# Attention + FP4 feed-forward on one core: the row maximum of two score banks taken as two steps of 512 columns and a join, instead of one step of 1024

## The reference, cut to what matters

```python
# attention, 4 batches x 1024 rows x 128; 16 heads of 64
m = jnp.max(s, axis=-1, keepdims=True)          # <- the row maxima of the scores
e = jnp.exp(s - m)
attn = e / (jnp.sum(e, axis=-1, keepdims=True) + EPS)
x = x + (attn @ v) @ Wo.T + bo                   # q, k, v from layernorm(x)
# then a gated feed-forward whose inputs and weights are rounded block by block to FP4
h = jax.nn.silu(fp4_linear(x, w_gate)) * fp4_linear(x, w_up)
x = x + fp4_linear(h, w_down)
```

## Time and profile before

| | |
|---|---|
| median of 3 runs | 1841.92 us (1841.74 to 1843.65) |
| the profiled execution | 1839.61 us, of which the span of the trace is 1837.8 us |
| TensorE busy, weight loads | 90%, 66% of the span |
| VectorE busy | 84% |
| GpSimd busy | 68% |
| ScalarE busy | 59% |
| TensorE clock granted, mean | 0.967 of full speed |
| max steps, `sm` matmuls | 512 and 1024 |

### The profile page before, as it was taken

One profiled execution on the slowest core, in us unless ns is written; L12 is line 12 of the kernel. 1 busy time (PEld: TensorE's weight loads), 2 busy tenths in 40 slices (PEclk: granted clock), 3 DMA queues, 4 the chain that ended last, 5 costly groups with the idle time before them and its releaser, 6 DMA issues.

```text
span 1837.8 us, 41990 instructions
## 1 busy us (share of the span) xinstructions
PE 1649.2 (90%) x13825; PEld 1205.2 (66%) x13825; DVE 1544.5 (84%) x2591; ACT 1078.5 (59%) x2222; POOL 1241.5 (68%) x1369
## 2 busy tenths in 40 slices
PE   4899999999999989999999998989989898999966
PEld 2566677677666666666666666666666666766754
DVE  7888887777888979789797888888888888898877
ACT  3566666666656656566565565655656555666533
POOL 3577777777776766676666766666666666677753
PEclk7999999999999999999999999999999999999987
DMA  5111101111011110011110011100111000111000
GB/s 128 25 24 24 24 17 23 24 25 24 13 26 26 26 26 16 14 26 26 26 26 13 17 26 26 26 15 15 26 27 24 21 21 16 26 25 25 3 4 12
DMA packets 26424, 43.92 MB, mean 24 GB/s; under 512 B 3744, under 2 KB 18016, under 8 KB 26208
## 3 DMA queue, kind: packets, MB, share of 16 engines
q1 hardware_dynamic: 26208, 40.99, 10.1%
HBM read 4.80 MB, written 2.10 MB: 4 GB/s over the span
## 4 chain that ended last, share of the span: by engine, by line
POOL 34%; issue 28%; PE 19%; DVE 16%; ACT 2%; POOLq 1%; DMA 0%; DVEq 0%; ACTq 0%
POOL p_low L392 30%; PE ob L545 5%; DVE negm L773 4%; PE sm L499 4%; POOL o_n L399 3%; PE st L517 3%; PE st L519 3%; DVE q_hl L729 1%; PE mb L460 1%; DVE mhl L781 1%; DVE mhl L778 1%; PE mb L444 1%; PE mb L449 1%; DVE k_l L729 1%; POOLq L74 1%
## 5 line engine op out<-in xcount | busy, mean ns | idle before, releaser
L392 POOL TENSOR_TENSOR p_low<-probs 128x512 f16<-128x512 f32 x1024 | 1080.3, 1062 | 513.3 <-ACT probs L627 511.1
L627 ACT ACTIVATE probs<-st 128x512 f32<-128x512 f32 x1024 | 608.0, 597 | 472.3 <-PE st L519 467.3
L773 DVE TENSOR_REDUCE negm<-sm 128x1 f32<-128x1024 f32 x512 | 624.9, 1221 | 125.5 <-PE sm L499 120.6
L517 PE MATMUL st<-q_hl,k_hh 128*128 128x512 f32 x1024 | 467.8, 457 | 25.2 <-issue 25.0
L499 PE MATMUL sm<-k_hh,q_hl 128*128 128x512 f32 x1024 | 373.1, 446 | 90.4 <-DVE negm L773 85.1
L519 PE MATMUL st<-q_hm,k_l 66*128 66x512 f32 x1024 | 411.1, 401 | 0.0
L545 PEld LDWEIGHTS ob<-v,probs 128*128 128x128 bf16 x4096 | 241.3, 100 | 144.9 <-issue 134.3
L545 PE MATMUL ob<-v,probs 128*128 128x129 f16 x4096 | 331.2, 224 | 0.0
L545 PEld LDWEIGHTS ob<-v,p_low 128*128 128x128 f16 x4096 | 234.0, 97 | 142.8 <-issue 131.4
L545 PE MATMUL ob<-v,p_low 128*128 128x129 f16 x4096 | 321.9, 221 | 1.7 <-POOL p_low L392 1.7
L517 PEld LDWEIGHTS st<-q_hl,k_hh 128*128 128x128 f32 x1024 | 195.4, 191 | 68.3 <-issue 28.4
(11 more groups left out here) (146 smaller groups left out, 1671.2 us busy)
## 6 DMA issues: line engine op xcount, KB each, us to landing
k_hh<-k_hh SPq DMA_DIRECT2D x64, 256.0 KB, 3.6
q_hm<-q_hl SPq DMA_DIRECT2D x64, 256.0 KB, 3.7
q_hm<-m_row SPq DMA_DIRECT2D x256, 2.0 KB
x<-x SPq DMA_DIRECT2D x4, 512.0 KB, 7.2
out<-x SPq DMA_DIRECT2D x24, 64.0 KB, 1.5
probs<-wq SPq DMA_DIRECT2D x1, 512.0 KB, 5.5
probs<-wk SPq DMA_DIRECT2D x1, 512.0 KB, 6.7
probs<-wv SPq DMA_DIRECT2D x1, 512.0 KB, 7.1
```

What stands on the lines that cost most here:

```text
L392: return pool.tensor_tensor(p_low[b][:, j, :], p, p.bitcast(BF16)[:, 1::2], ALU.subtract)
L517: pe.matmul(st[s % 2][:, :], k_hh[n][:, s * P:(s + 1) * P], q_hl[n][:, half * HALF:(half + 1) * HALF], start=True, stop=False)
L627: nc.scalar.activation(probs[k % 2][:, s, :], st[s % 2][:, :], ACT.Exp, scale=SCALE).then_inc(s_ex, 1)
L773: nc.vector.tensor_reduce(negm[k % 2][:, s // 2:s // 2 + 1], sm[:, :, :].rearrange("p a n -> p (a n)"), AX.X, ALU.max, negate=True).then_i ...
```

## The change

The one max step over 1024 columns becomes two over 512 columns, one per bank, each released by its own `sm` matmul and each writing a column of a new small tile `negm_half`. At the end of a unit a further small reduction takes 4 minima over 2 columns (the values are negated maxima) into `negm`, and `mhl` is made from that. TensorE's wait before a `sm` matmul is now one for each bank: for the step on that bank two slots back, instead of one wait ahead of each pair.

```diff
+        negm_h = [sb(f"negm_half{n}", [P, IT, 2]) for n in range(2)]
+        s_mc = sem("max_halves_joined")
 # TensorE, scores(s)
-                        if s % 2 == 0:
-
-                            wait(pe, s_mx, 4 * (unit + 2) + s // 2)
+
+                        wait(pe, s_mx, 8 * (unit + 2) + s - 1)
 # VectorE, round_
-                        if has_max and s % 2:
+                        if has_max:
                             wait(dve, s_sm, 8 * (unit + 2) + s + 1)
-                            nc.vector.tensor_reduce(negm[k % 2][:, s // 2:s // 2 + 1], sm[:, :, :].rearrange("p a n -> p (a n)"),
+                            nc.vector.tensor_reduce(negm_h[k % 2][:, s // 2, s % 2:s % 2 + 1], sm[:, s % 2, :],
                                                     AX.X, ALU.max, negate=True).then_inc(s_mx, 1)
                         if has_max and s == SLOTS - 1:
 
-                            wait(dve, s_mx, 4 * (unit + 3))
+                            wait(dve, s_mx, 8 * (unit + 3))
+                            nc.vector.tensor_reduce(negm[k % 2][:, :], negm_h[k % 2][:, :, :], AX.X, ALU.min).then_inc(s_mc, 1)
+
+                            wait(dve, s_mc, unit + 3)
                             nc.vector.tensor_scalar(mhl[:, 0, :].bitcast(F32R), negm[k % 2][:, :], LIFT, None, ALU.add
                                                     ).then_inc(s_nm, 1)
```

## The result

The changed kernel takes **1963.16 us** (median of 4 runs, 1957.99 to 1966.89) against 1841.83 us for the kernel before, a ratio of 1.0657 (95% interval 1.0625 to 1.069). The prediction said 1949 us, 1888 to 1998. The profiled execution has a span of 1958.1 us, 120.3 us more than before.

What follows compares the result with a forecast made beforehand. TensorE and VectorE were taken to lead by turns within a round. Losses of 31.5, 10.2, 54.3, 21.2 and 7.5 less 17.6 make 107 us on 1839.6; with 2.3 for the median, 1949 us, range 1888 to 1998.

Steps and rivals of the forecast that it cites:

- Part 1: VectorE's max steps: halves add 0.07 us per pair, joins 26 us (at most 88); 1.9 us more per round.
- Part 2: TensorE's sm pairs after late max steps: earlier bank 0 release saves 0.20 us each, 97 steps, some 19 us at most.
- E: Duration of VectorE's other work in an even slot, queued behind the half step; for example 3.45 us in (2,2).
- Part 3: Even slots: VectorE's work now starts after scores plus half step, delaying TensorE by 0.34 to 1.05 us at six places.
- P: Start of a pair of sm matmuls; the half step's follower was to start at P + 1.10 us.
- The sum: Whole kernel: place losses less 17.6 us given back, plus 7.5 for first rounds and the rest, make 107 us.
- Throughput alone: Rival: waits are caught up elsewhere, only VectorE's added 1.9 us a round reaches TensorE; 1862 to 1903 us, chance 0.14.
- Faster: Rival: VectorE reaches even slots late anyway, so only the earlier release acts; 1815 to 1830 us, chance 0.05.
- no change: Rival: losses and gains in the kernel cancel within 0.2%; chance 0.04.
- The clock falls: Rival: a 1.9 us stand in (3,6) halves TensorE's clock in 23 rounds, costing 60 us; 2009 us, chance 0.10.

Runs made afterwards that it cites:

- e2: Kernel before, with a wait for the pair's first scores and a one-column memset heading each even slot, wide step kept; 1989.52 us, ratio 1.0789.
- e1: Changed kernel with bank 0's half step behind VectorE's other work in all sixteen even slots; 1850.4 us, ratio 1.0049.
- e3: Kernel before, wide step kept, plus the join's small reduction on a constant tile ahead of the mhl steps; 1840.51 us, ratio 0.9997.
- e5: As e1, but TensorE waits once ahead of each pair, for both half steps; 1845.04 us, ratio 1.0023.
- e10: Kernel before with half steps at five pairs per round only, bank 0's behind the slot's work, per-bank waits there, join kept; 1846.79 us, ratio 1.0027.
- e6: Changed kernel, but TensorE waits once ahead of each pair, for both half steps; 2092.27 us, ratio 1.1342.
- e12: Changed kernel with bank 0's half step behind the slot's work in ten even slots, still ahead at the six predicted places; 1945.2 us, ratio 1.0544.
- e8: Changed kernel with bank 0's half step behind the takes of g and u in slot (3,2) alone; 1959.71 us, ratio 1.0634.

## Why the prediction was right, step by step

The forecast of 107 us against 121 measured has the right mechanism, but that the number came so near is in part luck: two errors of some 30 us each, with opposite signs, are in it, as said under the sum.

**The kind** was right: the cost is what stands behind the early wait. e2 has the wait without the work, and is slower than the change; e1 and e3 have the work without the early wait, and cost 9 us and nothing.

**Part 1** was right in its prices (0.69 for 0.68, 0.16 for 0.17) and wrong in the sum "VectorE gets 1.9 us more per round": it got less busy. The half steps added 65 us (690.3 against 624.9) and the join 20.6; but the small steps that make `mhl` fell from 792 and 453 ns to 429 and 357, and of the FP4 steps more fell than rose (line 933 from 658 to 347 ns; line 952, which `x` waits for, rose from 499 to 973). In the trace of before the first of the `mhl` steps is long (0.57 to 1.0 us for four columns) in 102 of 128 cases; each of these starts inside a GpSimd instruction and ends within 0.03 us of that one's end. The 26 of 0.17 us all start when GpSimd is idle. With the change 46 are long in the same way, and 82 are short: 51 start when GpSimd is idle, 31 in the last 0.13 us of its instruction. So VectorE's steps now fall elsewhere in GpSimd's work. That waiting for TensorE shifts them there is the likely reason; no run isolates it. On the Trainium skill ("SBUF — State Buffer", "Who interferes with whom"): the trace agrees for the join, whose mean is 161 ns, while the `tensor_scalar` behind it is still at 429 with a shortest of 0.17.

**Part 2** was right in kind, and its gain does not reach the total. "TensorE then has one `sm` matmul left to do after the wait instead of two" is what happens. Where the half steps follow each other, e1 against e5 shows 1.2 us for it in a written-out round and some 11 us in the whole kernel, against the 19 at most; the second stand at the loop's edge and the clock take it back, and in e10, which has no such stand, the busy time of the pairs does. In the change itself the separate release is not worth 19 us but 129 (e6), because there the steps are E apart. The prediction had counted it in its place-by-place sums (it used the second matmul of the pair), so the sum did not suffer.

**Part 3**, place by place, measured in the round shown against the prediction's loss:

| place | new release, predicted | measured | loss predicted | measured |
|---|---|---|---|---|
| `t0` behind `q0`, (0,6) | P + 2.69 | P + 2.91 | 1.05 | 1.27 |
| `m` behind `o1`, (2,0) | P + 1.84 | P + 1.94 | 0.34 | 0.44 |
| second `sm` behind (2,2) | P + 5.29 | P + 4.94 | 0.54 | 0.19 |
| `x` behind (2,6) | P + 3.2 to 3.3 | P + 3.20 | 1.0 | 0.91 |
| `m` behind `u`, (3,2) | P + 2.31 | P + 2.39 | 0.82 | 0.90 |
| second `sm` behind (3,4) | P + 4.77 | P + 3.99 | 0.92 | 0.14 |

Four are right to 0.25 us. (At `u` the prediction left the 0.06 of its own rule out of the sum; with it the release is P + 2.37, and 2.39 was measured.) Two at FP4 steps were too large in this round, because E was taken as it was before: in (2,2) it was 3.45 us and is now 3.08, in (3,4) it was 2.93 and is now 2.14, by the shorter small steps:

```profile
621.51 0.51 DVE L928 TENSOR_REDUCE q_small<-xn 128x22 f32<-128x352 f32 x1
622.05 0.18 DVE L930 TENSOR_SCALAR q_small<-q_small 128x22 f32<-128x22 f32 x1
622.26 0.18 DVE L933 TENSOR_SCALAR q_small<-q_small 128x22 f32<-128x22 f32 x1
622.48 0.29 DVE L935 RECIPROCAL q_small<-q_small 128x22 f32<-128x22 f32 x1
622.80 0.92 DVE L937 TENSOR_TENSOR qv<-xn,q_small 128x352 f32<-128x352 f32 x1
623.65 0.68 DVE L774 TENSOR_REDUCE negm_half<-sm 128x1 f32<-128x512 f32 x1
```

In the six rounds in which the small steps of (3,4) are long, the second matmul starts at P + 4.95, and there the predicted P + 4.77 is nearly right. The six places sum to 3.85 us in the round shown instead of 4.67. The round from one pair of (3,2) to the next is 56.81 us (560.07 to 616.88); before, from 541.61, the next such pair is this one in the timeline of the kernel before, 54.30 later:

```profile
595.91 0.71 PE L499 MATMUL sm<-k_hh,q_hl 128*128 128x512 f32 x2
```

So a round that is written out costs 2.5 us more, where the prediction had 3.9. The six places lose 3.85, of which 1.35 come back, where the prediction had 0.8: TensorE reaches its stands in units 0 and 1 later. That is no gain of the new order there, for e12, which has it in these units at (0,6) alone, is 18 us faster than the changed kernel.

**The sum** came out near because a second term was missing. In the looped rounds, two per iteration, VectorE's first step of a round stands at 1055.40 and 1167.52 in the kernel before and at 1116.75 and 1239.06 in the changed one: 112.1 us per iteration against 122.3, 10.2 more and not 2 x 2.5. At the loop's edge the changed kernel has a second stand for no engine (10.6 us in 9 times, 0.8 to 1.4 each) and a longer stay of the clock at its lower level. The windows of the changed kernel there:

```profile
1173.00:1176.00 3.00, 0.58 (x1) 0.50 (x2) 0.76 (x1) 0.00 (x0) 0.74 (x1) 0.77 0.01 3
1176.00:1179.00 3.00, 1.64 (x11) 1.04 (x10) 0.16 (x1) 0.60 (x1) 1.04 (x1) 0.50 0.03 8
1179.00:1182.00 3.00, 3.00 (x15) 2.01 (x15) 2.12 (x6) 0.60 (x1) 0.43 (x1) 0.50 0.02 5
1182.00:1185.00 3.00, 3.00 (x15) 1.91 (x14) 0.00 (x0) 1.89 (x4) 0.61 (x1) 0.53 0.00 0
```

and the stand inside the second of them:

```profile
1175.42 0.79 PE L518 MATMUL st<-q_hl,k_hh 128*128 128x512 f32 x1 [2.96 <-issue]
...
1178.56 0.48 PE L546 MATMUL ob<-v,probs 128*128 128x129 f16 x3 [1.36 <-issue]
```

Before, the clock was low in three windows, 0.60, 0.50 and 0.76; now in four. e5 shows that the second stand goes when TensorE's list has one wait per pair again, so it comes from the list; in e1, which keeps both waits and has no early step, it is there too (9.3 us), and so is a clock of 0.965. That is 1.4 us of stand in this iteration, and by the mean clocks (0.041 of 1958.1 against 0.033 of 1837.8) at most some 20 us of TensorE's time in the whole kernel, since part of the slow time falls on stands. So the prediction lacked a term of some 30 us, and its losses per round were too large by nearly as much in sum. Per iteration the second stand (1.4) and one more low window (3.4 us at half speed, 1.7) explain 3.1 of the 5.2 us that go beyond two rounds of 2.5. Most of the rest is in the choice of marks. From TensorE's first `sm` pair of a round to that of the round after next, the iteration takes 112.83 us before (1053.89 to 1166.73) and 122.32 with the change (1116.32 to 1238.64), 9.5 more; a written-out round taken the same way is 2.7 longer (54.30 and 57.00). That leaves 4.1 us beyond two such rounds, all at the edge: 1.7 between the pairs of (3,6) and (0,0), and 2.35 between those of (0,0) and (0,2). Besides the stand and the low window they hold a give-back that is missing: a written-out round gets 1.2 us back before the pair of (0,2), where TensorE stood in the kernel before, but it stood there in 12 rounds only, and not in those just behind the edge. The three sum to 4.3 us.

**The rivals.** "Throughput alone" falls with e1 and e3. "Faster" and "no change" fall with the result. "The clock falls" was partly there, but less often than in every round: its price is at most the 20 us above, against the 60 I gave it. Its condition, a stand of 1.9 us at the pair of (3,6), came in six rounds only (2.03). Away from the edge the clock fell in three looped rounds of the changed kernel, each time about 1 us behind the stand of 1.5 to 1.6 us for `x` (at 1099.5, for instance); the same stand in the other rounds was followed by no fall, and no run shows what decides. On the rule of the Trainium skill ("TensorE: Matmul & The Clock Gate", "Why this matters for your kernels"): the traces agree that long stands are followed by the lower level, but they show falls behind a stand of 1.53 us (e8) too, which is shorter than the gaps that section warns of; the measurement decides. Of what the profile was to show, VectorE's wait at the steps (330 us, I said near 200), the three stands of the jobs and `x` at 1.56 came; the stand of 1.9 us at `sm` came in six of 23 rounds (2.03, else 1.07), and a round of 58 us is 56.8 written out and 61.2 in the loop.

What stays open: why the second wait per pair brings the second stand there; and how much of e2's excess is the clock (0.956) and how much the wide step.

## What to carry to other kernels

A wait is paid by all that stands behind it on its engine. Before a step is cut in two, ask where the first half's wait will stand, and which takes and which other engine's buffers are queued behind it: here the same instructions with the half step behind the slot's work cost 9 us and ahead of it 121. If a step is cut in two, its consumer's wait must be cut too when other work lies between the halves (129 us here). When they are adjacent it is worth little: 1.2 us in a written-out round, and nothing in the whole kernel.

The sum of stands that a profile shows is not time gained until the busy time is compared as well: a wait that moves inside a pair of matmuls is counted as work (e1, e10), and so is a lower clock (e8).

## What was not expected of the hardware

- VectorE was busy for less time with more instructions: small steps between SBUF tiles took 429 ns in the mean instead of 792 (line 782, 778 before) when VectorE waited more for TensorE. The long ones of line 778, 102 of 128, all ended with the GpSimd instruction in which they started; with the change 46 did.
- With one more wait per pair on TensorE a stand of 0.8 to 1.4 us (up to 1.9 in some runs), "issue", comes soon after the loop's edge, 9 times; it is in all runs that have these waits at every pair and absent in the kernel before, e2, e3, e5, e6 and e10.
- TensorE's clock was granted at its lower level in the middle of a round, after 1.47 us of work in 3.00 and a single stand of 1.53 us (e8).
